# Score products of the 8-wide and 16-wide heads, one per head and in turns between two row groups, in a decoder of 16 attention stages

## The reference: what is computed

```
x = ln(x + L0_attn(x))            # 16 heads of 8, causal, rotary
x = ln(x + L0_xattn(x, ctx))      # one head of 128
x = ln(x + L0_ffn(x))             # 9 experts, gated
x = ln(x + L1_attn(x))            # 4 layers: 4 local heads and 4 linear heads of 16, and an MLP
x = ln(x + L1_xattn(x, ctx))      # 16 heads of 8, 77 keys, no mask
x = ln(x + L1_ffn(x))             # 8 experts
x = ln(x + L2_attn(x))            # 16 heads of 8, causal
x = ln(x + L2_xattn(x, ctx))      # two attentions of 16 heads of 32, two MLPs
x = ln(x + L2_ffn(x))
x = ln(x + L3_attn(x))            # 16 heads of 8, causal, relative positions
x = ln(x + L3_xattn(x, ctx))
x = ln(x + L3_ffn(x))             # 16 heads of 8, no mask, then 8 experts
```

## Time and profile before

| | before |
|---|---|
| median of the timed runs | 5704.05 us (5701.13 to 5717.39, 3 runs) |
| the profiled execution | 5674.14 us |
| its span, first to last instruction | 5672.6 us |
| TensorE matmuls busy | 5110.4 us (90%), 27990 instructions |
| loads of the stationary operand | 2613.1 us, 27990 instructions |
| VectorE / ScalarE busy | 2829.6 / 3051.5 us |
| mean granted TensorE clock | 0.962 of 2.4 GHz |

### The profile page before, as it was taken

One profiled execution on the slowest core, in us unless ns is written; L12 is line 12 of the kernel. 1 busy time (PEld: TensorE's weight loads), 2 busy tenths in 40 slices (PEclk: granted clock), 3 DMA queues, 4 the chain that ended last, 5 costly groups with the idle time before them and its releaser, 6 DMA issues. The chain is left out here.

```text
span 5672.6 us, 81045 instructions
## 1 busy us (share of the span) xinstructions
PE 5110.4 (90%) x27990; PEld 2613.1 (46%) x27990; DVE 2829.6 (50%) x6564; ACT 3051.5 (54%) x11252; POOL 23.6 (0%) x34
## 2 busy tenths in 40 slices
PE   7999988889799998888889999888898999989889
PEld 4444445544444444554344444455434444445443
DVE  5255555562525555556253545555625255555562
ACT  5444565564544456656454445665645444466564
POOL 0000000000000000000000000000000000000000
PEclk9989999999999999999999989999999999999999
DMA  1100000000010000000001000000000100000000
GB/s 37 41 6 6 18 18 12 5 1 15 25 41 6 6 21 18 9 5 1 19 25 37 6 6 20 18 9 5 1 19 22 41 6 6 23 16 9 5 1 19
DMA packets 22511, 85.93 MB, mean 15 GB/s; under 512 B 2512, under 2 KB 3024, under 8 KB 21968
## 3 DMA queue, kind: packets, MB, share of 16 engines
q1 hardware_dynamic: 22096, 80.58, 4.4%
HBM read 78.47 MB, written 2.10 MB: 14 GB/s over the span
## 5 line engine op out<-in xcount | busy, mean ns | idle before, releaser
L1051 ACT ACTIVATE work<-bank,rowmax 128x128 f32<-128x128 f32 (+1 forms) x4096 | 1395.1, 395 | 306.7 <-DVE rowmax L1366 305.9
L1051 ACT ACTIVATION_READ_ACCUMULATOR work<-bank,rowmax 128x1 f32 x4096 | 989.1, 244 | 0.0
L1366 DVE TENSOR_REDUCE rowmax<-bank 128x4 f32<-128x512 f32 (+2 forms) x1152 | 610.8, 578 | 458.8 <-PE bank L677 346.6
L694 PE MATMUL bank<-ident,work 128*128 128x128 f32 (+1 forms) x4096 | 658.2, 289 | 134.5 <-DVE probsT L1425 101.9
L542 PE MATMUL bank<-mask_causal,identb 128*128 128x512 bf16 x2368 | 676.3, 394 | 40.1 <-issue 28.7
L694 PEld LDWEIGHTS bank<-ident,work 128*128 128x128 f32 (+1 forms) x4096 | 488.6, 148 | 349.1 <-DVE probsT L1425 172.5
L1164 ACT ACTIVATE work<-bank,small 128x512 f32<-128x512 f32 x544 | 371.8, 688 | 490.1 <-PE bank L883 490.1
L910 PE MATMUL bank<-work,slot 128*128 128x512 f32 x1344 | 611.7, 592 | 0.0
L1621 DVE SCALAR_TENSOR_TENSOR part<-bank,small,sq 128x512 f32<-128x512 f32 x192 | 144.1, 751 | 785.0 <-PE bank L910 775.4
L1425 DVE COPY probsT<-bank 128x512 f32<-128x512 f32 (+2 forms) x832 | 479.6, 600 | 68.7 <-PE bank L694 64.9
L677 PE MATMUL bank<-km,q 32*128 32x512 f32 (+2 forms) x1792 | 426.2, 570 | 19.3 <-ACT work L1051 11.9
(11 more groups left out here) (266 smaller groups left out, 6226.6 us busy)
## 6 DMA issues: line engine op xcount, KB each, us to landing
slot<-in_w_stream SPq DMA_DIRECT2D x68, 512.0 KB, 3.4
slot<-in_w_stream SPq DMA_DIRECT2D x32, 768.0 KB, 3.9
slot<-in_w_stream SPq DMA_DIRECT2D x32, 384.0 KB, 3.1
small<-in_w_small SPq DMA_DIRECT2D x1, 2288.0 KB, 9.0
x<-in_x SPq DMA_DIRECT2D x8, 256.0 KB, 3.6
out<-x SPq DMA_DIRECT2D x8, 256.0 KB, 2.0
ctx<-in_ctx SPq DMA_DIRECT2D x8, 77.0 KB, 3.4
```

The source lines that it names most:

```text
L694: ins = nc.tensor.transpose(b[0:nk, j * P:(j + 1) * P], probs[t % 2][:, r, j, 0:nk], ident[:])
L1051: ins = nc.scalar.activation(probs[t % 2][:, r, j, 0:nk], banks.where(("scores", n, c, s, r))[:, j * nk:(j + 1) * nk], ACT.Exp, bias=rowma ...
L1366: V.tensor_reduce(m[:, 4 * r:4 * r + J], banks.where(("scores", n, c, s, r))[:, 0:J * nk] .rearrange("p (j k) -> p j k", j=J), AX_X, ALU.m ...
```

## The change

Instead of one product of J x nk columns for each row group, the scores are now made with one product of nk columns for each head, j outermost and the two row groups of the pair inside. Each product names the same stationary operand, and loads it again. The event `scores` comes with the last product of each row group, as before.

```diff
                                 else:
-                                    for r in pair:
-                                        g32 = slice(32 * r, 32 * r + 32)
-                                        nc.tensor.matmul(banks.where(("scores", n, c, s, r))[:, 0:J * nk],
-                                                         B["q"][c][g32, s * P:(s + 1) * P], km[c][g32, s, 0:J, 0:nk],
-                                                         start=not st["mask"], stop=True
-                                                         ).then_inc(*made("scores", (n, c, s, r)))
+                                    for j in range(J):
+                                        for r in pair:
+                                            g32 = slice(32 * r, 32 * r + 32)
+                                            ins = nc.tensor.matmul(banks.where(("scores", n, c, s, r))[:, j * nk:(j + 1) * nk],
+                                                                   B["q"][c][g32, s * P:(s + 1) * P], km[c][g32, s, j, 0:nk],
+                                                                   start=not st["mask"], stop=j == J - 1 or not st["mask"])
+                                            if j == J - 1:
+                                                ins.then_inc(*made("scores", (n, c, s, r)))
```

## The result

| | before | after |
|---|---|---|
| median of the timed runs | 5697.28 us (5686.24 to 5717.39, 6 runs) | 5806.5 us (5792.48 to 5821.3, 6 runs) |
| ratio, 95% interval | | 1.0202 (1.0179 to 1.0224) |
| the profiled execution, mean granted clock | 5674.14 us, 0.962 | 5792.48 us, 0.942 |
| its time at 1.2 GHz (clock events of the trace) | 432 us | 674 us |
| mean time at 1.2 GHz of all executions | 476 us (75 runs) | 707 us (6 runs) |

The changed kernel is slower by 109 us, not by 20, and the time lies outside the range of 5697 to 5754. The last row is worked out from each run's granted clock: (1 - clock) x 2 x time, since the clock has two levels, 1.2 and 2.4 GHz. The 75 have a mean of 5686.6 us, and after is 120 us above that.

The account below looks back on a forecast made before the run. It took the masked loop from second pair through VectorE's row maxima to the next pairs as the bound. Terms of 5.8, 12, 0.6 and 1.3 us made about 20, added to 5704 for 5724 us (+0.35%), range 5697 to 5754.

Parts of the forecast that it names:

- The loop that a masked pair is part of: Masked attention: second pair, VectorE row maxima, turned-block copy, remaining turns, next mask, next pairs; each pair's change counts once.
- the prices of all pairs: Score pairs: +0.03 us with 128 keys (1.16), +0.33 with 77 (1.12), two in flight 1.64, 16-wide +0.01.
- 16-wide pair: Layers L1_0 to L1_3: a pair, 0.70 us before, changes by -0.05 to +0.03, taken +0.01; 1.3 us in all.
- L1_xattn "2.5 to 3.5 us longer each time": Sign in the profile after: the 77-key stage grows this much each pass; under 1 us would refute the forecast.
- The sum of "about 20 us": Whole kernel: 5.8 masked 8-wide stages, 12 L1_xattn, 0.6 L3_ffn, 1.3 L1 layers; bounds 2 and 35.
- Hidden after all: Rival in L1_xattn: ScalarE's idle time absorbs the first pair's loss, so +8 us, 5712; chance 0.19.
- narrow products onto a mask dearer: Rival in masked stages: each pass 0.02 us longer on a mask-filled bank, 31 and 10 us more, 5765; chance 0.08.
- turns that open an overlap: Rival on the masked path: alternating row groups opens missing overlap, saving 0.5 us a pair, 5628; chance 0.02.
- The loads of a pair: Score pairs: eight stationary-operand loads in a row group make an estimated 0.86 us before any tail.
- the step that gave the clock a place only in the L1 layers: L1 attention stages: 55 us hang on where the clock falls; gaps stay as they are, so little change expected.
- some 12 either way: Whole kernel: the clock's share of the forecast's own spread, in us, beside terms between 8 and 33.
- The rival on the clock: L1 layers' attention: more passes and loads might keep TensorE at 2.4 GHz, 5669; faster by this, chance 0.08.

Follow-up runs that it names:

- x_full128: Kernel before with one product per head in L1_xattn alone, each streaming 128 columns instead of 77; 5688.49 us, ratio 1.0004.
- the three parts: Kernel before with the new loop in L1_xattn, the masked 8-wide stages or the 16-wide layers alone; 5710.87, 5735.9 and 5688.24 us.
- lin_only: Kernel before with the new loop in the four L1 layers (16-wide heads) alone; 5688.24 us, ratio 0.9996.
- after_late3: Kernel after with three extra overwritten products in the MLP ahead of L2_a2, to move that stage later; 5782.8 us, 1.0188 of before.
- after_late1: Kernel after with one extra overwritten product in the MLP ahead of L2_a2, to move that stage later; 5772.51 us, 1.0179 of before.
- wide_l2_shift2: Kernel after with the old wide products in L2_attn and two more unread products in each later item there; 5832.01 us, 1.0255 of before.
- after_warm12: Kernel after with 12 instead of 4 unread products at the head of L2_a2; 5776.72 us, 1.0150 of before.
- before_lin_warm: Kernel before with one unread product ahead of the second turned block of each item in the L1 layers' attention; 5650.32 us, ratio 0.9931.
- before_lin_warm2: Kernel before with two unread products in each turned block of the stages with 16-wide heads; 5632.14 us, ratio 0.9906.

## Why the prediction was wrong

Right, by its own steps:
- The loop that a masked pair is part of, and the prices of all pairs: 1.16, 1.12 and 1.64 us as read from L670; 0.71 for the 16-wide pair, forecast 0.71 (0.70 and 0.01).
- L1_xattn "2.5 to 3.5 us longer each time": 3.1 with the clock at 1.00 in `x_full128` (62.1 for 59.0, with pairs of 1.16 in place of 1.12); 4.5 in after, of which about 1.3 are the price of 3.4 us at the low clock (0.38 each).
- The sum of "about 20 us": 19.4 at an equal clock from the three parts, good to some 5 us. After itself has 29.9. The difference need not be a further term of the pairs: L2_a2's low clock costs 0.43 us per us (16.3 for 37.5) where the column takes off 0.39, and L2_a2 has 126 us more of it than before, which makes 5. That is an argument; no run separates it.
- Hidden after all, narrow products onto a mask dearer, and turns that open an overlap: none of the three came. The 16-wide pair is within 0.01. The loads of a pair, an estimated 0.86 us for eight in a row group, take 0.97 in the trace after (55.24, PEld of L678), and the pair is 1.16 as forecast.

Wrong: the step that gave the clock a place only in the L1 layers and "some 12 either way" in the whole. Low clock rose by 231 us from the mean of the 75 runs, and 231 x 0.38 = 88 of the 120 us between those means are that (in the two profiles 242 x 0.38 = 92 of 118). The rival on the clock looked at the one kind of stage where the rows of before had much of it, and reasoned that gaps which stay the same leave the clock the same. It called TensorE the less dense engine there, which its own row does not bear out (27.78 busy of 30.70 us, VectorE 25.04). The L1 layers have 195 us of low clock in the profile before and 201 after, so between these two that rival's stage hardly moved; but over the profiles of the other kernels without unread products there it is 123 (`lin_only`) to 321 (`after_late3`), 27 us of time less to 48 more, so 12 was too small even for the stage that was looked at. L2_a2 had at most 10.2 us a pass in the profile before, and the prediction has no row of it for the clock; it went to 37.5 in four of four. `after_late1` and `wide_l2_shift2` show that products of less than 1 us ahead of the stage take this away or bring it back, which no sum over the edited products contains. And in L1_xattn the 3.4 us come with the narrow products themselves, as `x_full128` shows; there the stage before had a clock of 1.00 in every pass, and the prediction set no term of the clock on it.

By measured parts the slowdown of 118 us between the two profiles is: pairs, 19 to 20; the low clock of L2_a2, 56.5 in the profile; L1_xattn's, about 5; L2_attn's and L2_a1's, 19.5 less 2 for the pairs, 17 to 18; the rest, some 20 us, is spread over the other stages and is not taken apart here.

Open: why the clock stays low for 37.5 us in a stretch where TensorE has hardly a gap and comes back behind twelve unread products in `after_warm12`, and why starts of the stage within 0.3 us give 10.2, 13.7 or 37.5. The runs show when it happens, not by what rule. That the four passes of after all meet the bad place while those of before meet none is also only observed; with L2_attn's narrow products in place the stages from L2_attn to L2_a2 had the same low stretches in each pass to 0.2 us, which `before` has not.

## What to carry to other kernels

Price a change by its products and then, by itself, by the clock: look up the granted clock of every stage downstream, and of every execution, since a kernel of untouched stages can lose more to it than the edit costs (here about 88 us against 20). When a change of a few tenths of a us makes an untouched stage 16 us longer, test the shift and not the edit: unread products ahead of the stage tell place from cause, and inside a stage that often runs at the low clock they can be worth more than what they cost (one in `before_lin_warm`, 0.993 of before; two in `before_lin_warm2`, 0.991).

## What the runs showed of the hardware

- TensorE kept 1.2 GHz for 37.5 us in 14 of 68 passes of the same 715 records of L2_a2; in the pass of after read here, 23 us of them had no gap between matmuls. With twelve unread bf16 products at the head of the stage (`after_warm12`) it was back after 13.7 us, in four of four.
- In those 68 passes the place where the clock falls sorts how long it stays low: 13.7 us up to 0.90 us behind the stage's beginning, 37.5 at 0.95 to 1.20, 10.2 from 1.25 to 2.25.
- The spread of 1% between executions of one kernel here goes with the clock: over 75 runs of before, 5653.79 to 5731.56 us, the time follows the low time at 0.38 us per us, with 3.4 us of scatter left (standard deviation).
- Two row groups' float32 pairs of 16 passes over 128 columns take 1.16 us and over 77 columns 1.12; in L1_xattn the ones over 77 bring a low stretch 24 us into the stage (35 of 36 passes), those over 128 don't (none of 4).
- An unread product of 0.2 us in each item raised L1_0 from a clock of 0.84 to 0.93 to one of 1.00: it takes 68.0 us each pass there, 70.6 to 75.8 before. Over the sixteen layer passes low clock went from 195 to 41 us.
